# A fused chain of attention layers in fp32: activations loaded in blocks for VectorE to turn, and the engines' order rewritten

## The reference, cut to what matters

```
# layer 0: causal self attention, cross attention, feed forward; 16 heads of 16
mask0 = 1 - all(x == 0, axis=2)                      # one flag a row
x1 = layernorm(x + mha(x, x, Wq1, Wk1, Wv1, mask0, causal=True))
mask1 = 1 - all(x1 == 0, axis=2)
x2 = layernorm(x1 + mha(x1, context, Wq2, Wk2, Wv2, mask1))   # K, V of context rows times mask1
x3 = layernorm(x2 + (relu(x2 @ fc1.T + b1) * mask0 @ fc2.T + b2) * mask0)
# inside mha: lengths = sum(energy[:, :, 0, :] != 0); columns >= lengths are masked
# layer 1: "pair": F = layernorm(x3), N = layernorm(context)
att = softmax(F @ N.T * 256**-0.5) @ N
cross = gelu(att @ fc1.T + b) @ fc2.T + b
nc = layernorm(cross); sa = softmax(nc @ nc.T * 256**-0.5) @ nc
x4 = F + gamma2 * (cross + gamma1 * sa)
# layer 2: "real"
x5 = x4 + softmax(x4 @ context.T) @ context
# layer 3: "mix": 8 heads of 32 over layernorm(x5) and layernorm(context), then a recurrence
x6 = x5 + mha(layernorm(x5), layernorm(context))
U = (layernorm(x6) @ W_in.T + b_in) @ Bmat
s = silu(s @ A.T) + U[:, t]        # 128 steps, one after the other
out = x6 + states @ Cmat + mod     # mod: one row a sequence
```

## Time and profile before

| | us |
|---|---|
| timed runs (3) | 4104.85, 4111.22, 4113.52 |
| median | 4111.22 |
| span of the profiled execution | 4106.6 |

### The profile page before, as it was taken

One profiled execution on the slowest core, in us unless ns is written; L12 is line 12 of the kernel. 1 busy time (PEld: TensorE's weight loads), 2 busy tenths in 40 slices (PEclk: granted clock), 3 DMA queues, 4 the chain that ended last, 5 costly groups with the idle time before them and its releaser, 6 DMA issues. The chain is left out here.

```text
span 4106.6 us, 111739 instructions
## 1 busy us (share of the span) xinstructions
PE 3913.2 (95%) x37177; PEld 3233.6 (79%) x37177; DVE 3349.2 (82%) x9519; ACT 3547.9 (86%) x8460; POOL 2854.5 (70%) x3172
## 2 busy tenths in 40 slices
PE   6899999999999999999999999999999999999859
PEld 5688888888888888888888888888888888887647
DVE  4788888888888888888888888888888888888635
ACT  4799999999998999999899999989999998999635
POOL 2577777777777777777777777777777777777636
PEclk7999999999999999999999999999999999999969
DMA  3001011011101101110110111011011101100038
GB/s 115 22 29 34 20 31 34 20 34 31 34 20 31 34 21 33 31 34 20 31 34 23 31 31 34 20 31 34 23 32 31 34 20 31 34 24 28 18 80 306
DMA packets 121876, 159.94 MB, mean 39 GB/s; under 512 B 12296, under 2 KB 108450, under 8 KB 116642
## 3 DMA queue, kind: packets, MB, share of 16 engines
q1 hardware_dynamic: 116896, 145.39, 11.5%
q10 hardware_dynamic: 4416, 7.41, 0.5%
HBM read 114.86 MB, written 37.75 MB: 37 GB/s over the span
## 5 line engine op out<-in xcount | busy, mean ns | idle before, releaser
L618 PE MATMUL bank<-ident,prob 128*128 128x128 f32 x5120 | 728.8, 277 | 56.9 <-ACT CR L1005 26.9
L938 ACT ACTIVATE probT<-bank 128x512 f32<-128x512 f32 x1280 | 730.6, 593 | 59.6 <-PE bank L618 56.7
L909 ACT ACTIVATE turned<-bank 128x512 f32<-128x512 f32 x896 | 538.7, 601 | 186.9 <-PE bank L554 177.8
L618 PEld LDWEIGHTS bank<-ident,prob 128*128 128x128 f32 x5120 | 590.9, 142 | 138.4 <-issue 48.8
L1138 DVE TENSOR_REDUCE mx<-bank 128x4 f32<-128x512 f32 x768 | 507.9, 682 | 187.3 <-PE bank L589 184.7
L927 ACT ACTIVATE prob<-prob,mx 128x128 f32<-128x128 f32 x2048 | 650.6, 396 | 4.1 <-DVE mx L1127 4.0
L562 PE MATMUL bank<-turned,shared 128*128 128x256 f32 x2560 | 616.4, 384 | 1.2 <-ACT turned L909 1.1
L1444 POOL TENSOR_TENSOR rs_ln<-ve_ln,half 128x2 f32<-128x2 f32 x320 | 227.3, 710 | 446.8 <-DVE ve_ln L1109 446.8
L1149 DVE TENSOR_TENSOR prob<-bank,mx 128x512 f32<-128x512 f32 x768 | 520.7, 685 | 15.3 <-PE bank L618 1.9
L562 PEld LDWEIGHTS bank<-turned,shared 128*128 128x128 f32 x2560 | 469.8, 191 | 69.0 <-issue 12.3
L919 ACT ACTIVATE prob<-prob 128x512 f32<-128x512 f32 x768 | 475.5, 636 | 13.0 <-DVE prob L1149 12.1
(11 more groups left out here) (238 smaller groups left out, 9071.8 us busy)
## 6 DMA issues: line engine op xcount, KB each, us to landing
shared<-in_x SPq DMA_DIRECT2D x128, 256.0 KB, 2.9
CB<-in_ctx SPq DMA_DIRECT2D x64, 256.0 KB, 4.0
CC<-in_ctx SPq DMA_DIRECT2D x64, 256.0 KB, 2.7
mod<-mod_rows SPq DMA_DIRECT2D x64, 256.0 KB, 3.8
residual<-X SPq DMA_DIRECT2D x64, 256.0 KB, 3.1
out<-turned SPq DMA_DIRECT2D x16, 1024.0 KB, 4.8
turned<-residual SPq DMA_DIRECT2D x14, 1024.0 KB, 7.1
u_turned<-us SPq DMA_DIRECT2D x124, 32.0 KB, 2.2
```

The source lines that it names most:

```text
L618: last = nc.tensor.transpose(t[:, h * 128:(h + 1) * 128], src[:, h, :], ident[:])
L909: nc.scalar.activation(dst, banks.of(f"{unit}.{name}")[:, 0:n], ACT.Copy).then_inc(*st["act"].mark(name))
L938: nc.scalar.activation(flat(t), banks.of(f"{att}.turn.{b}{r}")[:, :], ACT.Copy).then_inc(*st["act"].mark(f"probT.{b}{r}"))
```

## The change

- `x` and `context` are also loaded in blocks: four DMAs a load (`in_blocks`), one for each 32 partitions, in pieces of 32 floats. DVE turns each 128x512 tile in one `transpose` of 32x32 blocks (`x_turned`, `ctx_turned`). PE's steps `xT`, `cT`, `ccT`, `CT` and ACT's evacuations of them are gone. The turned context (`ccT`, three buffers) serves the mask, the normed context and `real`.
- The flags of x1 (`kept`) and the scale and shift of the context norm (`norm`) are written to DRAM and read back as rows broadcast over the partitions (`rowout`, `rowin`). POOL multiplies and adds with them: `mask` (one product in place of two), `hcs`, `HCT`.
- V stays in PSUM until `vp`; `valid` is written into VP; `nz` counts by itself; `count`, `spread`, `nm` and X1r are gone. The pair scaling sits in `n1_scaled` and in `ncT`. The flags lie in rings of four, X1 in two buffers.
- All lists of `PROGRAM` and all of `BANKS` are rewritten; `PREPARED` is 2 in place of 3.

```diff
+    x_q, ctx_q = (t.rearrange("(g b) (k c) (a j i) -> g j c a b k i", b=G, c=32, j=4, i=32) for t in (x_d, ctx_d))
...
+                def in_blocks(t, src, g, here):
+                    v = t[:].rearrange("p b d -> p (b d)").rearrange("p (a b k i) -> p a b k i", a=DH, b=G, i=32)
+                    for j in range(4):
+                        sp.dma_start(v[32 * j:32 * j + 32], src[g, j]).then_inc(here.sem, 16)
...
+                def kept_to(g):
+                    for w in latest(kept_in.before(g), ctx_in["dve"].done("keep", g)):
                         sp.wait_ge(*w)
+                    sp.dma_start(kept_d.rearrange("(b s o) -> s b o", b=G, o=1), keep1[g % 4][:].unsqueeze(2), allow_slow_non_contiguous=True)\
+                        .then_inc(kept_out.sem, 16)
+
+                def kept_from(g):
+                    for w in latest(kept_out.done(g), ctx_in["pool"].before("mask", g)):
+                        sp.wait_ge(*w)
+                    sp.dma_start(kept_row, kept_d.partition_broadcast(128)).then_inc(kept_in.sem, 16)
...
+                def x_turned(g):
+                    waits_apart(dve, prep, *latest(x_in.done(g), *(self_in["pe"].before(n, g) for n in "qkv")))
+                    nc.vector.transpose(flat(trn["XT"]), x_blocks.rearrange("p b d -> p (b d)")).then_inc(*self_in["dve"].mark("xT"))
+
+                def ctx_turned(g):
+                    for w in latest(ctx_in2.done(g), real["pe"].before("screal", g, 3), ctx_in["pool"].before("mask", g, 3),
+                                    pair["pool"].before("hcs", g, 3)):
+                        dve.wait_ge(*w)
+                    nc.vector.transpose(flat(ccT[g % 3]), flat(nat["CB"])).then_inc(*ctx_in["dve"].mark("cT"))
...
                 def mask(g):
+                    for w in latest(kept_in.done(g), ctx_in["dve"].done("cT", g), ctx_in["pe"].before("k", g), ctx_in["pe"].before("v", g)):
+                        pool.wait_ge(*w)
+                    nc.gpsimd.tensor_tensor(trn["CBT"][:], ccT[g % 3], kept_row.unsqueeze(1).to_broadcast([128, DH, W]), ALU.mult)\
+                        .then_inc(*ctx_in["pool"].mark("mask"))
+
+                def hcs(g):
+                    for w in latest(norm_in.done(g), ctx_in["dve"].done("cT", g), mix_in["pe"].before("k", g), mix_in["pe"].before("v", g),
+                                    pair["dve"].before("NXT", g)):
+                        pool.wait_ge(*w)
+                    nc.gpsimd.tensor_tensor(trn["HCT"][:], ccT[g % 3], norm_row[:, 0, :].unsqueeze(1).to_broadcast([128, DH, W]), ALU.mult)\
+                        .then_inc(*pair["pool"].mark("hcs"))
...
     "sp": """
-        mix_out.load@6 ctx_in.load@3 pair.load@4 self_in.load@0 mix_out.store@6 mix_out.store_u@6 self_att.load@1
+        pair.rowin@4 self_att.load@2 self_in.load@0 pair.load@2 mix_out.load@5 pair.rowout@3 mix_out.store@6
+        ctx_in.load@2 mix_out.store_u@6 ctx_in.rowout@2 ctx_in.rowin@2
     """,
```

More of the change, by code:

```diff
@@ L140 @@
     "pe": """
[L141 to L155, removed]
@@ L158 @@
+        ctx_att.scores.12@3 real.h5T@5 self_att.back.1@2 ctx_att.turn.01@3 pair.FT@4 mix_in.v@4 pair.sc1@4
+        ctx_att.turn.00@3 mix_in.q@5 ctx_att.turn.02@3 pair.pT1@4 ctx_att.turn.03@3 self_in.e0@1 pair.av1@4
+        mix_out.u@6
     """,
     "act": """
-        self_att.outT.1@3 ctx_att.exp.03@4 real.h5T@6 ctx_att.probT.01@4 pair.FT@5 ctx_att.exp.00@4 ctx_att.exp.11@4
-        mix_in.v@5 ctx_att.exp.02@4 pair.exp1@5 ctx_att.probT.00@4 ctx_att.exp.12@4 mix_in.q@6 pair.pT1@5
-        ctx_att.probT.03@4 ctx_att.probT.02@4 pair.gelu@5 self_att.ln1@3 pair.cross@5 ctx_att.exp.13@4
@@ L168 @@
[L168 to L172, removed]
+        self_att.outT.1@3 ctx_att.exp.01@4 ctx_att.exp.00@4 real.h5T@6 ctx_att.probT.01@4 pair.FT@5
@@ L173 @@
+        self_att.probT.13@2 self_att.probT.12@2 pair.lnF@4 self_in.q@1 mix_out.h6T@6 real.ln5@5
     """,
     "dve": """
[L175 to L193, removed]
+        ctx_att.max.10@4 pair.lnNstats@5 mix_att.centre.03@6 pair.lnNaggr@5 ctx_att.centre.10@4 pair.lnNve@5
@@ new lines @@
+        ctx_in.amax@3 ctx_in.keep@3 mix_att.sum.02@6 mix_att.recip.02@6 mix_in.k@5 mix_att.max.00@6
+        mix_att.max.01@6 mix_att.centre.00@6 mix_att.sum.03@6 ctx_att.recip.0@4 mix_att.recip.03@6
+        ctx_att.norm.0@4 ctx_att.recip.1@4 ctx_att.norm.1@4 mix_att.sum.00@6 mix_att.centre.01@6
+        mix_att.recip.00@6 self_in.valid@2 ctx_in.cT@3 ctx_att.ln2stats@4 ctx_att.ln2aggr@4 ctx_att.ln2ve@4
+        pair.mx2@5 mix_att.sum.01@6 mix_att.recip.01@6 self_att.mask.01@2 pair.lnCaggr@3 self_att.max.01@2
@@ new lines @@
+        self_att.mask.00@2 pair.rs2@5 self_att.max.00@2 self_att.mask.03@2 ctx_in.q0@3 pair.sa@5
+        self_att.max.03@2 self_att.mask.02@2 self_att.max.02@2 self_att.mask.10@2 ctx_in.nz@3 self_att.mask.11@2
+        ffn.relu@4 self_att.max.10@2 self_in.vp@2 self_in.amax@2 self_att.max.11@2 ffn.sum@4 ffn.ln3stats@4
+        ffn.ln3aggr@4 real.mxreal@5 ffn.ln3ve@4 self_in.keep@2 real.rsreal@5 mix_out.res@6 ctx_in.valid@3
+        mix_out.ln6stats@6 self_in.xT@1 self_att.mask.13@2 mix_out.ln6aggr@6 self_att.mask.12@2
@@ L194 @@
+        ctx_att.centre.12@3 pair.rs1@4 pair.part1@4 self_att.ln1stats@2 self_att.ln1aggr@2 self_att.ln1ve@2
+        ctx_att.max.13@3 self_in.nz@1 pair.lnCstats@2 mix_out.u@6 ctx_att.centre.13@3 mix_att.max.02@5
+        mix_att.max.03@5 mix_att.centre.02@5
     """,
     "pool": """
-        real.x5b@6 self_att.ln1gain@3 self_att.ln1@3 pair.lnNpow@5 pair.lnNnmr@5 ctx_in.mask@3 mix_att.part.02@6
-        pair.lnNgain@5 pair.lnN@5 ctx_att.add@4 mix_att.part.03@6 mix_att.part.00@6 ctx_att.ln2pow@4
+        pair.lnCpow@4 pair.lnCnmr@4 self_att.ln1pow@3 self_att.ln1nmr@3 ffn.biased@4 real.x5b@6
@@ L198 @@
+        self_att.ln1gain@3 self_att.ln1@3 pair.lnNpow@5 pair.lnNnmr@5 mix_att.part.02@6 pair.lnNgain@5
+        pair.lnN@5 mix_att.part.03@6 ctx_att.add@4 mix_att.part.00@6 ctx_in.mask@3 ctx_att.ln2pow@4
         ctx_att.ln2nmr@4 mix_att.part.01@6 ctx_att.ln2gain@4 ctx_att.ln2@4 pair.skip@5 pair.gam2@5 pair.x4@5
-        ffn.x2b@4 ctx_in.keys@3 ffn.ln3pow@4 ctx_att.copies@3 ffn.ln3nmr@4 mix_out.ln6pow@6 mix_out.ln6nmr@6
-        ffn.ln3gain@4 ffn.ln3@4 ffn.copies@3 pair.lnCpow@4 pair.lnFpow@4 pair.lnCnmr@4 pair.lnFnmr@4 real.ln5pow@5
@@ new lines @@
+    mix_in.k:3 ctx_att.out.1:1 ctx_in.x1T:2 ctx_att.back.0:5 mix_att.turn.02:6 ctx_att.back.1:4
+    self_att.tile.00:2 self_att.tile.02:6 self_att.tile.01:0 pair.ncT:7 ctx_in.q:1 pair.sc2:6 mix_att.turn.03:4
+    ctx_in.k:3 pair.pT2:1 mix_att.turn.00:4 self_att.tile.10:7 self_att.tile.11:0 self_att.tile.03:5 pair.av:1
+    mix_att.turn.01:2 self_att.turn.01:4 ffn.x2T:3 mix_att.out.0:5 ctx_in.e0:2 ffn.fc1:3 self_att.turn.02:4
+    self_att.turn.00:1 real.x4T:7 ffn.fc2:3 self_in.len:3 self_in.v:5 real.screal:0 mix_out.o:7
@@ new lines @@
+    self_att.turn.03:7 self_att.turn.11:2 real.pTreal:0 ctx_att.tile.01:3 self_att.tile.13:6 self_att.tile.12:1
+    self_att.out.0:7 real.av:0 self_in.k:5 self_att.back.0:0 self_in.q:1 self_att.turn.12:3 self_att.turn.10:2
+    mix_out.h6T:3 self_att.turn.13:7 ctx_att.tile.00:6 ctx_att.tile.03:4 ctx_att.tile.02:5 ctx_in.len:5
+    ctx_in.v:2 self_att.out.1:7 ctx_att.tile.11:3 ctx_att.tile.13:1 ctx_att.tile.12:6 real.h5T:0 pair.FT:4
+    ctx_att.turn.01:5 mix_in.v0:2 mix_in.v1:0 pair.sc1:5 self_att.back.1:7 ctx_att.turn.00:7 mix_in.q:3
@@ L223 @@
+    ctx_att.turn.02:5 ctx_att.turn.03:6 pair.pT1:4 self_in.e0:3 mix_out.u:4 pair.av1:2
 """.split())
@@ L1184, in norm @@
                             dve.wait_ge(*w)
-                        keep = keep0[0] if p == "self" else keep1[1]
-                        for w in latest(self_in["dve"].done("keep", g) if p == "self" else ctx_att["pool"].done("copies", g)):
+                        keep = (keep0 if p == "self" else keep1)[g % 4]
+                        for w in latest((self_in if p == "self" else ctx_in)["dve"].done("keep", g)):
                             dve.wait_ge(*w)
@@ L1441, in go @@
                     def go(g):
-                        for w in latest(st["act"].before(key, g), st["dve"].done(key + "ve", g)):
+                        for w in latest(norm_out.before(g) if key == "lnC" else st["act"].before(key, g), st["dve"].done(key + "ve", g)):
                             pool.wait_ge(*w)
```

332 lines of the change are left out of this document (157 added, 175 removed).

## The result

The changed kernel takes 4588.85 us (median of 4 runs, 4578.75 to 4590.49) where the kernel before takes 4109.74 (median of 4): a ratio of 1.1155, 95% interval 1.1135 to 1.1176. That is 479 us slower; the forecast was 135 us faster, and its range ended at 4095. Three views of the changed kernel, in the order in which they answer.

The account below looks back on a forecast made before the run. PE's issuing was taken as the bound: 63 x (-2.0 - 0.3) = -145 us, +10 at the start, gave a span of 3972, so 3976 us; range 3915 to 4095.

Parts of the forecast that it names:

- What bounds the kernel: Steady part: PE's issuing sets the 59.70 us period; its three longest kinds of wait come to only 1.15 us.
- PE, -2.0 us: PE, each period: four groups of four transposes go, 1.76 to 2.24 us, middle taken as 2.0.
- its waits, -0.3: PE's waits, each period: -0.3 us, as mix_out.u between av1 and cross shortens the wait for gelu; bounds -1.15 to +0.6.
- DVE, 0.69 us a transpose: DVE: two added 32x32 block transposes of 128x512 at 0.69 us each; nine small operations go, net about nothing.
- POOL +2.0, hidden: POOL, each period: net +2.0 us less the copies on 43.2, under 46 of 57.4, so hidden.
- The price of a 128 B piece, 43 to 65 ns: DMA queue: x and context loads in 2048 pieces each take 5.5 to 8.3 us of the engines' time per load.
- The flag row's store: SP's queue before mask: 0.5 us issue and 2.2 us to landing, as the small u stores; then read back in 3.8.
- 2.4 of slack: Flag row to mask to ctx_in.k: the chain has 2.4 us to spare if the queues are clear.
- The norm rows "hidden": Norm scale and shift through DRAM: two stores and one read, wanted a third of a period later, so hidden.
- The first rival: SP's queue between context load and ctx_in.k: flag row late behind context pieces, kernel slower, 4291 to 4530 us; chance 0.11.
- Start, +10: Kernel start: preparation waits for loads queued behind x's small pieces, +10 us; bounds -5 and +25.
- End, 0: Kernel end: the scan input's early read waits for a later step but was 70 us ahead of need; 0, bounds +-10.

Follow-up runs that it names:

- no_row_store: The changed kernel with the flag row and norm rows stored for the first group only, still read back for every group: 4031.23 us.
- rows_turned: The changed kernel with flags and norm rows turned by DVE, stored in 128 B pieces, norm rows at the end of SP's list: 4017.33 us.
- ctx_wide: The changed kernel with the context loaded in 1 KB rows, 256 pieces in place of 2048: 4610.49 us.
- kept_spread: The changed kernel with each group's 256 flags stored 512 B apart in DRAM, still 4 B each: 4264.52 us.
- best_end: rows_turned with bias loads issued by ACT and the early scan-input read split, after group 61's u store and group 62's store: 3952.76 us.

## Why the prediction was wrong

- **What bounds the kernel: right.** Without the 4 B stores PE is busy 98.9% of the steady stretch (97.9% before) at a granted clock of 1.00, and the period follows what PE has to issue. The waits read for it were the three longest that come in every group; a single one of 16.5 us lies between them in the view.
- **PE, -2.0 us, and its waits, -0.3: right in sum.** The forecast period was 57.4; no_row_store has 57.19, rows_turned 57.11. By the windows at 2000 to 2500, PE's busy time fell by 1.9 us a period (58.4 to 56.6) and its idle time by 0.6 (1.27 to 0.63).
- **DVE, 0.69 us a transpose: right** (0.695 and 0.701, rows of the changed kernel below). The small ones that went paid for part of it only: DVE's busy time in no_row_store is 3415.3 us against 3349.2, 1.0 us a group more, where "about nothing, at most +1.7" was forecast. **POOL +2.0, hidden: right**, 391.28 / 500 x 57.19 = 44.8 us against 43.2.

```profile
L1213 DVE STREAM_TRANSPOSE shared<-CB 128x512 f32<-128x512 f32 x64 | 44.9, 701 | 2.0 <-DMA CB<-in_ctx 2.0
L1207 DVE STREAM_TRANSPOSE turned<-shared 128x512 f32<-128x512 f32 x64 | 44.5, 695 | 5.4 <-DMA shared<-in_x 5.4
```

- **The price of a 128 B piece, 43 to 65 ns: too high,** and it did no harm: ctx_wide has an eighth of the context's pieces and the same period. In rows_turned the queue's packets, most of them 128 B pieces, took 16.6% of 16 engines' 4012.3 us, which is 28.5 ns each:

```profile
q1 hardware_dynamic: 373920, 170.79, 16.6%
```

- **The flag row's store, "2.2 us to landing as the small u stores": the step that failed.** It took 7.7. The u stores were taken as the nearest row because they are small; by the form of their pieces (512 B each, apart) they are not near at all. The change's stores are the first in this kernel that put many short pieces into one short stretch, and no row of before bounds that. With 2.2 us (kept_spread) or 2.05 (rows_turned) the wait at the mask is nearly gone, as the sum had it. In the changed kernel store and read took 7.7 + 4.5 = 12.2 us where the sum had 0.5 + 2.2 + 3.8 = 6.5 (the 0.5 is the issue, which the 2.2 already holds). That is 5.7 us late against 2.4 of slack; PE waits 3.9.
- **The norm rows "hidden": failed.** Nothing waits for the rows read back, but while their stores are under way the context load behind them takes 7.72 us to issue, and PE's signals come late: 1.81 to 2.07 us a period alone.
- **The first rival named the right wait, a nearby time (4530) and the wrong cause.** Its sign, a wait of microseconds of PE for the mask in each period, came. Its mechanism, context pieces in front of the flag row, decided nothing; the row's own pieces did. That 4530 is near 4589 is luck.
- **Start, +10: 32.** In rows_turned it is 11. So 21 went with the longer pieces and the norm rows' new place in SP's list; in no_row_store, which still sends the first group's rows in 4 B pieces, it is 23.
- **End, 0: 58.** "70 us ahead of need" was true of the read's data (landed 21.8 us after 4381.79, the scan's first product at 4488.2), but not of what SP issues behind it. It is 58 in rows_turned too, so the 4 B stores have no part in it. The step did not name what is queued behind a wait of SP and behind 34 us of transfers, though the prediction did so for the flag row.

Against the forecast's span of 3972: 63 x (65.92 - 57.40) = 537, start 22, end 58, together 617, which is 4588.7 - 3972.

## What to carry to other kernels

Price a small DMA by its pieces and where they land, not by its bytes: a column of 256 scalars scattered into one 1 KB row of DRAM took 7.7 us here, and a 32x32 transpose of 0.2 us ahead of it made it 8 longer pieces and 2 us. Before a store or load moves, list what its queue has to do behind it: SP stood for 34 us behind a long transfer, and at the end of the kernel no other work hid it. When one suspect pays for a loss, undo it alone and then together with the next: here the two stores were worth 5.65 and about 2 alone, and 8.73 together.

## What the runs showed of the hardware

- 256 stores of 4 B into one 1 KB stretch of DRAM took 7.7 us from their issue to that of the read that waits for them (8.4 with no norm rows in front); 512 B apart, 2.2 us; 8 pieces of 128 B, 2.05 us from the first of four issues.
- A load of x, 2048 pieces of 128 B, is issued in 2.65 us, and each of its four parts lands in 2.4 (median); the context's parts land in 3.0 in rows_turned. With 1 KB pieces for the context the period was no shorter (66.18 against 65.92).
- With the 512 stores of the norm rows in each period, some 200 of PE's signals in a run reach ACT and DVE late (waits of up to 5.6 us), against 17 before; those of the other engines are late no more often than before. That it goes with these stores is shown; by what path PE's signals are held is not, and it was not tried.
- Behind the early read (3904 KB and twice 976 KB) the next issue on SP took 33.78 us; behind best_end's first part of it, 33 us later, 0.35. That a queue takes only so much ahead would explain it and was not measured.
